# VectorE's order of work in an LSTM woven into six transformer layers: a gate sum and two additions, and one floor, change places

## What is computed

```python
def step(carry, xw_t):                       # 1024 times, one after the other
    prev_h, prev_c = carry
    a = xw_t + prev_h @ Wh
    i, f, o = sigmoid(a[:, :H]), sigmoid(a[:, H:2*H]), sigmoid(a[:, 2*H:3*H])
    g = tanh(a[:, 3*H:])
    next_c = f * prev_c + i * g
    next_h = o * tanh(next_c)

q, k, v = split(shift_tokens(x) @ Wqkv)      # attention of one layer
q = l2norm(q) * qs;  k = l2norm(k) * ksc
q = q * cos * scale + rotate_half(q) * sin * scale
k = k * cos / scale + rotate_half(k) * sin / scale
x = softmax(8 * q @ k.T, masked to a window) @ v @ Wo + x

xn = layernorm(shift_tokens(x)) * g + bln    # feed-forward of one layer
a, gate = split(xn @ W1 + b1)
x = a * gelu(gate) @ W2 + b2 + x
```

## Time and profile before

| | us |
|---|---|
| median of 3 timed runs | 5177.27 |
| lowest and highest | 5176.47, 5178.69 |
| span of the profiled execution, first to last instruction | 5175.6 |
| TensorE busy in it | 4769.9 (92%) |
| VectorE busy | 3483.0 (67%) |
| ScalarE busy | 2608.7 (50%) |
| GpSimd busy | 1913.4 (37%) |

### The profile page before, as it was taken

How to read it: one execution, slowest core, us unless ns; L and a number is a source line. 1 busy time by engine, 2 the same in 40 slices (tenths; PEclk the granted TensorE clock), 3 DMA queues, 4 the chain that set the end, 5 groups by cost and what they waited for, 6 DMA issues and landing times.

```text
span 5175.6 us, 192189 instructions
## 1 busy us (share of the span) xinstructions
PE 4769.9 (92%) x79632; PEld 3728.4 (72%) x79632; DVE 3483.0 (67%) x14167; ACT 2608.7 (50%) x8192; POOL 1913.4 (37%) x2070
## 2 busy tenths in 40 slices
PE   4665699999999999999999999999999999999887
PEld 1445487777777787777777787777777787776666
DVE  8665577676676677677676677676676677676554
ACT  0112255555555555555555555555555555555654
POOL 3650233333333333333333333333333333334442
PEclk6555699999999999999999999999999999999999
DMA  3020122322322422322322422322322422323341
GB/s 131 2 88 0 38 83 81 117 86 88 114 83 80 124 82 81 117 85 87 113 84 81 123 82 81 116 86 84 117 84 80 122 83 81 117 85 106 109 130 48
DMA packets 311365, 463.54 MB, mean 90 GB/s; under 512 B 213264, under 2 KB 239888, under 8 KB 297616
## 3 DMA queue, kind: packets, MB, share of 16 engines
q1 hardware_dynamic: 310544, 451.92, 28.8%
HBM read 381.93 MB, written 69.93 MB: 87 GB/s over the span
## 4 chain that ended last, share of the span: by engine, by line
PE 63%; DVE 11%; issue 7%; POOL 4%; ACT 3%; POOLq 0%; DVEq 0%; ACTq 0%
PE mm L908 14%; PE gates L185 12%; PE st L1020 8%; PE gates L177 5%; PE dd L1020 4%; PE st L947 3%; PE pt L1047 3%; PE tt L920 3%; PE pt L1055 3%; PE pt L961 3%; DVE qk L1342 2%; POOL va L811 2%; DVE pr L1392 2%; PE dd L977 2%; PE st L989 1%
## 5 line engine op out<-in xcount | busy, mean ns | idle before, releaser
L796 POOL TENSOR_TENSOR turned<-raw,rotl 128x256 f32<-128x256 f32 x768 | 712.6, 943 | 1667.1 <-ACT raw L1139 1356.7
L908 PE MATMUL mm<-wqkv,xa 128*128 128x512 f32 x2304 | 1166.3, 618 | 12.3 <-DVE xa L1305 8.4
L185 PE MATMUL gates<-hp,whp 128*128 128x6 bf16 x28672 | 849.2, 165 | 22.1 <-DVE hp L230 22.1
L185 PEld LDWEIGHTS gates<-hp,whp 128*128 128x128 bf16 x28672 | 784.3, 96 | 56.8 <-DVE hp L230 29.4
L1190 ACT ACTIVATE pr<-st,nb,qn 128x128 f32<-128x128 f32 x1536 | 688.5, 464 | 36.7 <-DVE nb L1380 36.2
L192 ACT ACTIVATE state<-gsum 128x16 f32<-128x16 f32 x896 | 195.4, 218 | 1009.9 <-DVE gsum L200 1003.6
L908 PEld LDWEIGHTS mm<-wqkv,xa 128*128 128x128 f32 x2304 | 384.2, 193 | 241.6 <-issue 222.8
L200 DVE TENSOR_REDUCE gsum<-gates 128x16 f32<-128x48 f32 x896 | 183.1, 204 | 526.1 <-PE gates L185 526.1
L177 PEld LDWEIGHTS gates<-hp,whp 128*128 128x128 bf16 x14336 | 423.2, 96 | 141.5 <-issue 85.6
L177 PE MATMUL gates<-hp,whp 128*128 128x2 bf16 x14336 | 485.8, 163 | 26.2 <-DVE hp L215 26.2
L804 POOL TENSOR_TENSOR qn<-ss,power 128x8 f32<-128x8 f32 x192 | 320.6, 1670 | 496.7 <-DVE ss L1351 487.5
(11 more groups left out here) (135 smaller groups left out, 9778.8 us busy)
## 6 DMA issues: line engine op xcount, KB each, us to landing
wqkv<-in_Wqkv SPq DMA_DIRECT2D x288, 512.0 KB, 4.4
w<-in_W SPq DMA_DIRECT2D x48, 1364.0 KB, 6.1
wo<-in_Wo SPq DMA_DIRECT2D x48, 1024.0 KB, 4.9
w<-in_W SPq DMA_DIRECT2D x48, 768.0 KB, 4.5
kT<-k_windows SPq DMA_DIRECT2D x96, 256.0 KB, 5.4
va<-v_windows SPq DMA_DIRECT2D x96, 256.0 KB, 5.5
k_windows<-kT SPq DMA_DIRECT2D x96, 256.0 KB, 4.4
v_windows<-vb SPq DMA_DIRECT2D x96, 256.0 KB, 5.0
```

Source lines behind the costliest of these rows:

```text
L185: last = nc.tensor.matmul(g[:, m * PARTS * BATCH:(m + 1) * PARTS * BATCH], self.whp[:, p, k, m * P:(m + 1) * P], self.hp[:, k, :, :].rearr ...
L796: ins = nc.gpsimd.tensor_tensor(dst[:, :, a, :], src[:, :, 1 - a, :], tab[:, :, a, :].broadcast_to([P, 8, HALF]), ALU.mult)
L908: ins = nc.tensor.matmul(mm[c % 2][:, :], shifted(xa, y.b, k), wqkv[:, c, k, :], start=(k == 1), stop=(k == 0))
```

## The change

VectorE's list in a slot changes in two places; no instruction is added or taken away, and no other engine's list changes. In the fifth step `gate_sum` stood behind `fin_add(y, 0)` and `fin_add(y, 1)`, and now stands ahead of both; the first follows it directly, the second follows `cell`. `h_keep` (of the step before) thereby comes ahead of both additions as well. In the seventh step `rot_floor(y, 2)` stood between `h_full` and `h_second`, and now stands behind `h_third`.

```diff
                 row_inv(x, 3)
                 row_scale(x, 3)
-                fin_add(y, 0)
-                fin_add(y, 1)
                 h_keep()
                 gate_sum()
+                fin_add(y, 0)
                 uv()
                 cell()
+                fin_add(y, 1)
                 h_hi()
                 h_full()
                 h_second()
@@
                 standardise(x)
                 h_hi()
                 h_full()
-                rot_floor(y, 2)
                 h_second()
                 h_rest()
                 h_third()
+                rot_floor(y, 2)
                 gate_sum()
                 h_keep()
                 rot_sum(y, 3)
```

## The result

The changed kernel takes 5188.62 us (median of 11 runs, 5185.77 to 5193.16), the kernel before 5177.09 us (11 runs, 5172.86 to 5178.69): a ratio of 1.0025, with a 95% interval of 1.0016 to 1.0034. The change makes the kernel slower by 11.5 us. The prediction was 5185 with a range of 5168 to 5196, so the time lies inside it, 4 us above the figure. The loss is over the 0.2% (5187.6) that the prediction took as the border of "slower": it had given that case 0.32 and "between" 0.58.

A forecast was written before the change was run, and what follows sets the result against it. TensorE, busy 3950.56 of 4020 us, was taken as the bound. +0.16 - 0.07 = +0.09 us a slot over 84 slots gave +7.6 us on 5177.3, so 5185 us, range 5168 to 5196.

The forecast's parts named there:

- slower: Whole kernel: case of a time over 5187.6 us, more than 0.2% slower than before; chance 0.32.
- between: Whole kernel: case of a time from 5166.9 to 5187.6 us, within about 0.2% of before; chance 0.58.
- The two terms of the sum: Per slot: a cost of 0.16 us in the fifth step and a gain of 0.07 us in the seventh.
- Both edits meet the lock: Fifth and seventh steps: small two-input VectorE operations beside GpSimd's turns wait until a turn ends; without a turn, 0.16 us.
- Edit two: Seventh step, floor moved behind the parts of h: `h_second` meets the same turn, gain only 0.07 us a slot.
- the fourth rival: Small operations aren't caught by turns: the seventh step's wait goes, the fifth gains 0.05 us a slot; 5151 us, chance 0.07.
- Edit one: Fifth step, gate sum ahead of the additions: `h_hi` comes 0.16 us later and TensorE waits that much longer at line 177.
- The steps: Fifth step: gate sum 1.50 us earlier, `uv` and `cell` end with the two turns, second addition makes `h_hi` 0.16 later.
- the tanh: Fifth step: the gate tanh waits behind the copy of `take_p(x, 3)` on ScalarE, starting at about 2499.2, not 2498.4.
- Its bound on the other side: Fifth step: an earlier `h_hi` could gain at most 0.05 us, since line 177 already started just in time.
- The other turn of the lock: Fifth step: `cell` or the second addition gets ahead of the second turn; 0.18 to 0.24 us a slot slower, chance 0.19.
- The power doesn't keep VectorE out: Fifth step: VectorE's second addition needn't wait for GpSimd's 128x8 power; the opposite rival gave 5333 us, chance 0.02.

The follow-up runs named there:

- e1: Kernel before with only the fifth step's new order (gate sum ahead of both additions), floor where it was: 24.6 us slower than before.
- e6: Changed kernel with GpSimd's norm of piece 2 ahead of its two turns of piece 3: 8 us under the kernel before.
- e2: Kernel before with only the seventh step's floor moved behind the parts of h, fifth step as before: 10.7 us faster than before.
- e3: Changed kernel with the fifth step's second addition moved behind `h_third`: 23.6 us faster than the kernel before.
- e7: Kernel before with GpSimd's two turns of piece 1 ahead of its norm of piece 0: 98 us faster than before.
- e5: Changed kernel with GpSimd's two turns of piece 2 behind its norm of piece 1 and copy of v: slot without a clock fall 48.856 us; total not given.

## Why the prediction was right, and where its terms were off

The two terms of the sum came as forecast, each by the mechanism that was named, and their sum in the slots (8.4 us) is near the forecast 7.6. That the time also came out near is in part luck, since the clock was not in the sum: the medians leave it only some 3 us here, in e1 11.

- **Both edits meet the lock**: right, at every operation that the prediction named. The rule of the Trainium skill (SBUF — State Buffer, Who interferes with whom) says that a VectorE instruction with two SBUF inputs contends with a GpSimd instruction that reads SBUF, and that `tensor_reduce` never does. The traces agree: line 223 took 0.58 us beside a turn and 0.16 without (e6), and the sums of squares of line 1346 took 0.67 to 0.68 in all 384 rows of the changed kernel, 25 of which ran beside a turn.
- **Edit two**: predicted -0.07 us a slot, measured -0.09 (e2). That the whole 0.27 would go (the fourth rival) is excluded: it took another move, the turns' (e6), to free line 223.
- **Edit one**: predicted +0.16, measured +0.16 (e1). The two edits together give 0.10 a slot and not the sum of the two runs, 0.07; that 0.03 stays unexplained. The steps hold to 0.02 us, bar the tanh, which came 0.07 earlier than I put it (I left out that ScalarE's next instruction starts before the one ahead has ended); the turn hid that.
- **Its bound on the other side was wrong**. I bounded what an earlier `h_hi` could give at 0.05 us, as line 177 started 0.08 behind line 173, and wrote that line 185 has no wait of its own. It has one, for the third part of h, hidden under the modelled 0.55 us of line 177. An earlier `h_hi` moves the third part too: e3 gained 0.08 in the fifth step and e7 0.19. For the same reason the waits of the fourth step, 0.31 us in the view, were worth 0.61. The sum was not hurt, as the third part moves by as much as `h_hi`.
- **The other turn of the lock** didn't come: `cell` was caught by the second turn, as in the earlier trace rows.
- **The clock** was not in the sum. The price of a slot was taken 84 times and the granted clock as a constant 0.99. Four more stretches at half clock are 6.4 us of the profiled difference, nearly as much as the sum that I had forecast (7.6). The slots alone make 0.16%, so the clock most likely put the result past the 0.2%; that isn't shown, as the falls behind the median are not counted. e1 lost 24.6 us where its slots make 13.
- **The power doesn't keep VectorE out**: right. The addition took its 0.68 us inside it. It is the power that grew, to 2.16 us, and in e3, without the addition beside it, it takes 1.64.

**What stays open** is what sets the number of falls. In the runs on the old GpSimd list it rose with the slot (17 at 48.221 us to 32 at 48.542), but 47.859 us had 1, 47.533 had 10 and 47.340 had 18. Each count is from one execution. What was shown is their place, their price of 1.4 to 1.6 us, and that in e5 they moved to the place behind the 0.94 us wait, in 46 slots.

## What to carry to other kernels

Moving an operation into a wait pays only if everything behind it is released by it: here the gate sum came 1.50 us earlier and the result 0.17 later, since another engine's list and a lock held the steps between. Where VectorE and GpSimd share work, look first at which GpSimd instruction runs beside the critical small operations, and move that one: two lines in GpSimd's list gave 98 us, and no order of VectorE's alone tried here gave more than 24. Price a wait of TensorE by the distance between the starts of its instructions with and without it, not by the idle time in a view: small matmuls can cover a wait with their own modelled length.

## What the runs showed of the hardware that was not expected

- A caught VectorE instruction can lose twice in a row. The store of h on 128x4 elements stood for 1.34 us beside two turns (e5), and `cell` for 1.18 us beside a copy and a product (e6), where in the earlier trace rows the two queues took turns.
- A matmul of 128x2 stands in the trace for 0.16 us, but one starts every 25 ns, so a wait that leaves 0.15 us without a start between two groups shows as no idle time. Line 185 started 0.06 us behind the end of the third part of h where that came last (e3), and 0.40 us behind the start of line 177 where it had come early (e5, e7).
- TensorE's granted clock fell from its upper level (2.4 GHz) to its lower one (1.2 GHz) for about 3.4 us in kernels in which TensorE is busy 97 to 98% of the time by the view, 1 to 46 times, at 1.4 to 1.6 us each.
